# Attention over channels on one core: Gram block, column sums and the read of y in another order, with y read by ScalarE alone

## The reference

```python
g = group_norm(x)                      # 8 groups of 2 maps, over s, c and the 2 maps
Q = einsum('oc,bscm->bsom', Wq, g) + bq    # 256 outputs each
K = einsum('oc,bscm->bsom', Wk, g) + bk
V = einsum('oc,bscm->bsom', Wv, g) + bv
QK = Qp @ Kt                           # per (b, m): 256 x 256, the sum runs over the 256 positions
A = softmax(QK, axis=-1)
out = einsum('bmcC,bmsC->bsCm', A, Vp) # sums A over its rows
y = x + einsum('oc,bscm->bsom', Wo, out) + bo
```

## Time and profile before

| | before |
|---|---|
| median of 3 runs | 189.87 us (188.49 to 194.72) |
| the profiled execution | 190.13 us |
| its span, first to last instruction | 188.1 us |
| PE, DVE, ACT, POOL busy | 161.7, 133.0, 130.2, 96.9 us |
| granted TensorE clock, mean | 0.893 of full speed |

### The profile page before, as it was taken

One profiled execution on the slowest core, in us unless ns is written; L12 is line 12 of the kernel. 1 busy time (PEld: TensorE's weight loads), 2 busy tenths in 40 slices (PEclk: granted clock), 3 DMA queues, 4 the chain that ended last, 5 costly groups with the idle time before them and its releaser, 6 DMA issues.

```text
span 188.1 us, 6983 instructions
## 1 busy us (share of the span) xinstructions
PE 161.7 (86%) x2672; PEld 93.6 (50%) x2672; DVE 133.0 (71%) x327; ACT 130.2 (69%) x533; POOL 96.9 (52%) x155
## 2 busy tenths in 40 slices
PE   7986969979799799979997899798989879999872
PEld 7765845524344464446444644463435435344541
DVE  4349359857469887888788777877898684678531
ACT  2001045975378969996998689968999999499721
POOL 1561385985386757675767476757274050007300
PEclk9999765555869999999999999999999995899996
DMA  6613974289289629962883297518935790002032
GB/s 220 179 37 72 228 213 179 39 191 236 112 162 196 213 30 205 226 233 36 186 202 151 29 200 154 201 24 202 227 124 82 195 265 35 0 0 115 2 137 89
DMA packets 10286, 26.46 MB, mean 141 GB/s; under 512 B 2731, under 2 KB 3726, under 8 KB 10254
## 3 DMA queue, kind: packets, MB, share of 16 engines
q1 hardware_dynamic: 8512, 25.16, 52.4%
q10 hardware_dynamic: 1742, 0.87, 1.8%
HBM read 8.85 MB, written 4.19 MB: 69 GB/s over the span
## 4 chain that ended last, share of the span: by engine, by line
PE 54%; ACT 14%; DVE 8%; issue 6%; POOL 3%; DVEq 0%; POOLq 0%
PE s_bank L449 15%; PE acc L473 14%; ACT e_sb L942 11%; PE bz L531 7%; ACT yb L954 3%; PE acc L431 3%; PE bx L379 3%; PE bx L389 2%; PE bz L437 2%; PE by L507 2%; DVE negmax L693 2%; PE bx L405 2%; DVE t_sb L682 1%; DVE t_sb L688 1%; PE by L515 1%
## 5 line engine op out<-in xcount | busy, mean ns | idle before, releaser
L942 ACT ACTIVATE e_sb<-s_bank,negmax 128x256 f32<-128x256 f32 x256 | 117.5, 494 | 25.0 <-DVE negmax L693 24.8
L693 DVE TENSOR_REDUCE negmax<-s_bank 128x2 f32<-128x512 f32 x128 | 84.8, 678 | 13.6 <-PE s_bank L449 13.1
L449 PE MATMUL s_bank<-stack,wq_st 99*128 99x512 f32 x128 | 56.8, 505 | 5.5 <-ACT e_sb L942 5.4
L942 ACT ACTIVATION_READ_ACCUMULATOR e_sb<-s_bank,negmax 128x1 f32 x256 | 57.8, 226 | 0.0
L449 PEld LDWEIGHTS s_bank<-stack,wq_st 99*128 99x128 f32 x128 | 23.3, 208 | 31.8 <-issue 31.5
L473 PE MATMUL acc<-e_sb,recip 128*32 128x256 f32 x512 | 37.6, 415 | 0.6 <-DVE recip L704 0.6
L1095 POOL TENSOR_TENSOR aR<-aT,coef 128x32 f32<-128x32 f32 (+1 forms) x16 | 3.6, 247 | 36.3 <-DVE aT L717 36.3
L1084 POOL TENSOR_TENSOR t_parts<-t_sb,t_parts 128x768 fp32r<-128x768 f32 (+1 forms) x14 | 21.7, 1552 | 1.1
L473 PEld LDWEIGHTS acc<-e_sb,recip 128*32 128x32 f32 x512 | 14.4, 115 | 15.0 <-issue 8.8
L1008 POOL TENSOR_TENSOR xc<-xs,nm 128x512 f32<-128x512 f32 x13 | 13.8, 1080 | 10.1 <-DVE nm L653 10.1
L954 ACT ACTIVATE yb<-bz,beff 128x256 f32<-128x256 f32 x16 | 6.7, 470 | 14.6 <-PE bz L531 14.6
(11 more groups left out here) (119 smaller groups left out, 199.2 us busy)
## 6 DMA issues: line engine op xcount, KB each, us to landing
stack<-t_parts SPq DMA_DIRECT2D x28, 256.0 KB, 5.0
stack<-t_parts SPq DMA_DIRECT2D x36, 128.0 KB, 5.0
xs<-x_rows SPq DMA_DIRECT2D x8, 512.0 KB, 4.9
xT<-x_cols SPq DMA_DIRECT2D x8, 512.0 KB, 5.6
y_cols<-yb SPq DMA_DIRECT2D x7, 512.0 KB, 5.2
stack<-t_parts SPq DMA_DIRECT2D x8, 32.0 KB
stack<-t_parts ACTq DMA_DIRECT2D x4, 64.0 KB, 3.5
stack<-t_parts SPq DMA_DIRECT2D x4, 64.0 KB, 2.7
```

What stands on the lines that cost most here:

```text
L449: nc.tensor.matmul(s_bank[q][:, :], wq_st[:, P * h:P * h + P], stack[:, b % 2, q, 2 * tt:2 * tt + 2, :].rearrange("p t n -> p (t n)"), sta ...
L693: nc.vector.tensor_reduce(negmax[:, n % NS, :], s_bank[n % NS][:, :].rearrange("p (i n) -> p i n", i=2), op=ALU.max, axis=AX.X, negate=Tru ...
L942: last = nc.scalar.activation(e_sb[:, s, i, :], s_bank[q][:, CH * i:CH * i + CH], ACT.Exp, bias=negmax[:, q, i:i + 1], accum_out=rowsum[:, ...
```

## The change: the order on PE, DVE and ACT

It does four things.

1. In the steady loop PE makes `column_sums(b, 0)` ahead of `gram_of(b + 3)` in slot 10; they stood the other way round.
2. DVE reads T's quarter 1 (in `bx`) in slot 8, right behind quarter 0, and the bias rows in slot 9; before, the bias rows came first and quarter 1 behind them in slot 9.
3. The second half of y is read by ACT behind the exponentials of slot 4, as two ACTIVATE of 128x256; before, DVE read it as one instruction of 128x512 behind the maximum of slot 5. The read at the very end of the program stays on DVE.
4. The Gram block of element 2 leaves the prologue and stands in slots 2 and 3 of element 0, behind T of element 1; what follows it in element 0 (variance 2, statistics of 3, T of 2, first column sums, Gram block of 3, variance 3) moves one or two slots back, and in element 1 the variance of 3 and the statistics of 4 stand a slot later.

```diff
-DVE_AT = dict(variance=0, invert3=1, groups=2, mean=4, acc=4, y23=5, invert0=6, a=6, t0=8, tb=9, t1=9, t2=10, t3=11,
+DVE_AT = dict(variance=0, invert3=1, groups=2, mean=4, acc=4, invert0=6, a=6, t0=8, t1=8, tb=9, t2=10, t3=11,
...
-ACT_AT = dict(y01=0)
+ACT_AT = dict(y01=0, y23=4)
...
             def gram_of(j):
-                if j >= 3:
+                if j >= 2:
                     pe.wait_ge(t_done, 4 * (j - 1) + 2)
...
             def t_product(j):
                 if j == 1:
-                    pe.wait_ge(gram_done, 3)
+                    pe.wait_ge(mean_done, 3)
                     pe.wait_ge(tb_done, 1)
...
+                    if s == (6 if last else PE_AT["sums0"]):
+                        column_sums(b, 0)
                     if b + 3 < B and s == PE_AT["gram"]:
                         gram_of(b + 3)
-                    if s == (6 if last else PE_AT["sums0"]):
-                        column_sums(b, 0)
...
             score(1)
-            gram_of(2)
-            sums_of(2)
             score(2)
...
+            def read_y23(k):
+                act.wait_ge(y23_mm, k + 1)
+                act.wait_ge(beff_done, k + 1)
+                after(act, y_stored[k % 2], 16 * (k // 2))
+                for i in range(2):
+                    last = nc.scalar.activation(yb[:, yb_of(k), 2 + i, :], bz[:, S * i:S * i + S], ACT.Identity,
+                                                bias=beff[:, 2 + i:3 + i])
+                last.then_inc(y23_read, 1)
...
                     if b >= 2 and s == ACT_AT["y01"]:
                         read_y01(b - 2)
+                    if b >= 2 and s == ACT_AT["y23"]:
+                        read_y23(b - 2)
```

More of the change, by code:

```diff
@@ L399, in variance @@
                     pe.wait_ge(set_blocks, 2)
-                if j == 2:
-                    pe.wait_ge(t_done, 4 + 2)
                 for k in range(2):
@@ L544, in element @@
                             tb_product(1)
+                        if s == 2:
+                            gram_of(2)
                         if s == 3:
+                            sums_of(2)
+                        if s == 5:
                             variance(2)
-                        if s == 5:
+                        if s == 7:
                             sum_rows(3)
-                        if s == 7:
+                        if s == 8:
                             mean(3)
-                        if s == 9:
+                        if s == 10:
                             t_product(2)
                             tb_product(2)
-                        if s == 11:
+                        if s == 12:
                             column_sums(0, 0)
-                        if s == 12:
+                        if s == 13:
                             gram_of(3)
-                        if s == 13:
+                        if s == 14:
                             column_sums(0, 1)
                             sums_of(3)
-                        if s == 15:
-                            variance(3)
                         continue
+                    late = 1 if b == 1 else 0
+                    if b == 1 and s == 1:
+                        variance(3)
                     if s == PE_AT["sums2"]:
                         column_sums(b - 1, 2)
-                    if b + 3 < B and s == PE_AT["rows"]:
+                    if b + 3 < B and s == PE_AT["rows"] + late:
                         sum_rows(b + 3)
-                    if b + 3 < B and s == PE_AT["mean"]:
+                    if b + 3 < B and s == PE_AT["mean"] + late:
                         mean(b + 3)
@@ L755, in element @@
                         if s == 1:
+                            read_t(1, 1)
                             read_tb(1)
-                            read_t(1, 1)
                         if s == 2:
@@ L761, in element @@
                             read_t(1, 3)
+                            diagonal_first(2)
                         if s == 4:
+                            read_gram(2)
+                            sum_diagonal(2)
+                        if s == 6:
                             read_variance(2)
-                        if s == 6:
+                        if s == 7:
                             sum_groups(3)
-                        if s == 7:
+                        if s == 9:
                             read_mean(3)
-                        if s == 9:
                             invert(0, 0)
-                        if s == 10:
+                        if s == 11:
                             read_t(2, 0)
-                            read_tb(2)
-                        if s == 11:
                             read_t(2, 1)
                         if s == 12:
-                            read_t(2, 2)
+                            read_tb(2)
                             invert(0, 1)
                         if s == 13:
+                            read_t(2, 2)
+                        if s == 14:
                             read_t(2, 3)
-                            read_gram(3)
-                        if s == 14:
                             invert(0, 2)
                         if s == 15:
-                            sum_diagonal(3)
+                            read_gram(3)
                         continue
-                    if b + 2 < B and s == DVE_AT["variance"]:
+                    late = 1 if b == 1 else 0
+                    if b == 1 and s == 0:
+                        sum_diagonal(3)
+                    if b + 2 < B and s == DVE_AT["variance"] + late:
                         read_variance(b + 2)
@@ L789, in element @@
                         invert(b - 1, 3)
-                    if b + 3 < B and s == DVE_AT["groups"]:
+                    if b + 3 < B and s == DVE_AT["groups"] + late:
                         sum_groups(b + 3)
-                    if b + 3 < B and s == DVE_AT["mean"]:
+                    if b + 3 < B and s == DVE_AT["mean"] + late:
                         read_mean(b + 3)
@@ L795, in element @@
                         read_acc(b - 1)
-                    if b >= 2 and s == DVE_AT["y23"]:
-                        read_y23(b - 2, bz)
                     if s == (5 if last else DVE_AT["invert0"]):
@@ L804, in element @@
                             read_t(b + 2, 0)
+                        if s == DVE_AT["t1"]:
+                            read_t(b + 2, 1)
                         if s == DVE_AT["tb"]:
                             read_tb(b + 2)
-                        if s == DVE_AT["t1"]:
-                            read_t(b + 2, 1)
                         if s == DVE_AT["t2"]:
@@ L903, in _ @@
             maximum(1)
-            diagonal_first(2)
-            read_gram(2)
-            sum_diagonal(2)
             dve.wait_ge(w_loaded, 16 * 4)
```

## The result

The changed kernel takes **200.54 us** (median of 4 runs, 198.03 to 204.31), against 189.52 (median of 4, 188.49 to 194.72) for the kernel before. The ratio of the two is 1.056, with a 95% interval of 1.042 to 1.070. The profiled execution took 200.67 us with a span of 198.9 (before 190.13 and 188.1), so the two spans differ by 10.8 us. Ratios here leave out executions that lie more than 1.5% above the fastest one of their kernel.

The account below looks back on a forecast made before the run. PE was taken to bound the steady elements, ACT element 5. Start -3.0, elements 2 to 4 +2.7, 5 to 7 +5.4 and clock falls +3.6 gave +8.7 on 190.1: 198.8 us, range 194 to 203, 189 to 206 for 8 in 10.

Parts of the forecast that it names:

- the clock: New clock falls where PE is sparse: two of five possible elements, 1.8 us each, +3.6 us, bounds 0 and 9.
- the start: Up to the end of element 1: Gram block of element 2 moved, waits shortened, -3.0 us, between -1.2 and -7.4.
- elements 5 to 7: ACT stands still for y with no Gram block to pay for it: 1.8 us each, +5.4 us, between 1.7 and 7.5.
- elements 2 to 4: T 2.0 us later, 1.1 us won at the Gram block, each element: +2.7 us, bounds -3.3 and +6.0.
- The stall: Behind slot 4 ACT idles 1.4 to 1.7 us for y's second half; T starts 2.0 us later, elements 2 to 4.
- The Gram block: Steady loop: first column sums fill PE's wait there, about 1.1 us won an element, 3.3 us over elements 2 to 4.
- Rival A: Clock falls in all elements, three more than forecast and each a little longer: 206 us, chance 0.12.
- B: ACT's wait for y's second half costs nothing; gains at the start and three Gram waits remain: 183.8 us, chance 0.16.
- C: Element 0's clock comes back ten microseconds sooner, winning 4.4 us: 190.8 us, no change, chance 0.17.

Follow-up runs that it names:

- second trace: The changed kernel run once more, unchanged: median 202.11 us, ratio 1.068 against the kernel before; the traced span is 200.5 us.
- the filled kernel: The changed kernel plus four products of zeros on PE between the scores of slots 8 and 9, elements 2 to 7: 193.94 us, ratio 1.037; again 197.56 us.
- first trace: The profiled execution of the changed kernel in its first runs: 200.67 us with a span of 198.9; median 200.54 us, ratio 1.056 against the kernel before.

## Why the prediction was right, step by step

The sum, +8.7 us for +10.8 measured (+12.4 in the second trace), held its sign and size. Its terms did less well than their sum: the clock was sized too low, the start and elements 5 to 7 too high, and that these errors partly cancel is luck. The second trace has one element 4 without a fall, and the filled kernel has elements 2 to 5 without one, so the terms can be told apart:

| term | forecast | first trace | second trace |
| --- | --- | --- | --- |
| start, without a low clock behind element 0 | -3.0 | -2.2 (taken from the second) | -2.2 |
| elements 2 to 4, without falls | +2.7 | +2.4 | +2.4 |
| elements 5 to 7, without new falls | +5.4 | +4.2 | +4.4 |
| falls of the clock | +3.6 | +6.0 | +7.5 |
| tail | 0 | +0.4 | +0.3 |
| sum | +8.7 | +10.8 | +12.4 |

(Elements 2 to 4: 3 x 19.75 less the 56.83 us of before. Falls, first trace: 71.10 - 67.64 = 3.5 at the start, 61.61 - 59.25 = 2.4 in elements 2 to 4, 0.1 in element 5. Second: 2.24 + 3.76 in elements 2 and 3, and 19.46 - 17.92 = 1.5 in element 5, whose 17.92 is the filled kernel's.)

*The stall.* Shown, nearly to the digit. ACT's idle time ahead of the read was forecast at 1.4 to 1.7 us and is 1.45 on the mean and 1.63 at most; the score of slot 9 waits 1.18 us for a forecast of 1.3; T comes 3.28 us behind y23 for a forecast of 3.7. Up to the start of slot 10's score the chain is the forecast's. The missing 0.45 us lies behind that score: I had added its 0.47 us and the issue gap of 0.38 behind it, and T in fact starts 0.41 behind the start of the score (102.23 and 101.82). That PE gets the next instruction ready while the score waits would explain it; the runs don't show it.

*The Gram block.* Shown: no wait of PE is left there, and the order alone wins 1.1 us an element. The steady element without a fall was to take 19.7 us, and takes 19.75.

*Elements 5 to 7.* Right in kind, somewhat large: +1.7, +1.1 and +1.5 us for a forecast of 1.8 each. Element 6, for which the prediction named room in ACT's list as its bound, paid the least.

*The start.* The term can't be read without the clock. The waits of DVE and ACT at the end of element 0 were to be "mostly gone", and half of each is left. Element 2 starts 2.2 us earlier at best in the two traces of the changed kernel, and 1.1 with the new start alone, whose time doesn't change by more than half a per cent. Over the four traces with the new start and no low clock behind element 0 it is 1.6 to 3.3 us earlier than before, so the 3.0 was possible and not the rule. The 0.9 us that I counted for a clock that stays up behind variance 3 is not borne out as a rule: of the ten traces with the new start, four have no low clock there, four one of 3.4 us, and two one of 13.7. Of the four traces with the old start one has 3.4 us and three have 17 to 24; that is too few to say whether the new start makes the long ones rarer.

*The clock.* The mechanism was named rightly: PE idle between single scores, then a fall, shown by the filler: with it none of the elements 2 to 5 has a fall in two traces, and without it seven of these eight have one. Its size was wrong twice. I took two falls at 1.8 us, +3.6. There were four new short ones in one trace, three at some 0.8 us and one at 0.1, and a long one behind element 0 at 3.5; and three in the other at 2.2, 3.8 and 1.5. The 1.8 came from element 6, a fall of 6.8 us; falls of that length cost 2.2 and 1.5 here, those of 3.4 us 0.9 at most, and one of 10 us 3.8, so a fall's price goes by its length, which no row of before gave for a dense element. Rival A, falls in all elements, was nearer in their number (four of the five that could have a new one, and three of five) than its chance of 0.12 says, but its 206 us are refuted by 200.5 and 202.1. The reading of the earlier trace rows has a slip too: the clock stands at 9 in the first four slices and again from slice 13 on, not from slice 11; nothing in the sum hangs on it.

*Rivals B and C.* B falls: the stall isn't hidden by the 2.39 us of ACT's slack at y01, which lies on the other side of it. That slack is still there, 12.0 us in eight waits. C isn't borne out either. The low clock of element 0 ends at 44.8 us in the changed kernel and at 48.7 in the kernel before, but at 43.2 to 44.3 in the three other traces with the old start, so the 4 us are not the change's.

*Where the read sits.* The Trainium skill says that ScalarE sits closer to PSUM (VectorE: DVE Perf Modes, Specifications). The runs show no gain from it: 0.84 us in two on ACT against 0.69 in one on DVE, and of the four places tried on ACT's list none with a lower median than with DVE.

**What stays open** is what sets the length and place of a fall, above all that behind element 0. It came with both starts, and in some executions of the same program and not in others. For slots 5, 6 and 7 the traces show when T starts (2.36, 1.53 and 2.27 us behind y23), but it was not measured how much of the differences between their medians is stall and how much clock.

## What to carry to other kernels

A read of PSUM moved to an in-order engine costs what that engine then waits for, not what the read takes: put it behind the last work that is ready before its producer ends, and ahead of the point where the producer's bank is wanted again. Here the medians were 200.5, 192.7, 187.3 and 188.3 us behind slots 4, 5, 6 and 7, not all on one chip. Slack that an engine shows elsewhere in the loop can't be drawn on across a point where the two engines meet.

A stall of an engine that isn't the bound may still cost PE its clock. When a price is put on that, ask how long the fall will last, take more than one trace of it, and try a few zero products in the gap before the order is changed: element by element, and not in the total, they show the two costs apart.

## What the runs showed of the hardware

- The clock went to 1.2 GHz behind a stretch in which PE was busy for 1.57 of 3.20 us, with waits of 1.18 and 0.45 us, and 1.05 us of zero products in it kept it at 2.4 GHz, in elements 2 to 5 of both traces with them. The stall alone doesn't decide it: element 4 of the changed kernel's second trace has the same waits (1.19 and 0.45 us) and no fall.
- Once low, it stayed so for 3.4 us or for 7, 10 or 13.5, with PE 100% busy by its records in the last two. So PE was busy by its records for 13.5 us without the clock coming back.
- The same program's low clock lay at other places in two executions (from 51.6 us on for 13.7 us in one; from 77.4, 101.3 and 142.3 us on for 7, 10 and 7 in the other), with mean clocks of 0.853 and 0.855.
- One traced execution, that of the order and the read behind slot 6 with the old start, had a clock of 0.85 for most of its span where the other traces had 1.00. The kernel ran on one core.
- The issue gap of 0.38 us behind the score of slot 10 was not there when PE had waited 0.45 us for ACT ahead of that score.
